# A step of a windowed attention stage in another order on four engines, and its masks laid by 32-row tiles

## The reference

```python
for i in range(DEPTH):                       # DEPTH = 6
    x = attn_layer(shift_tokens(x), Wqkv[i], q_scale[i], k_scale[i], Wo[i]) + x
    x = ffn_layer(shift_tokens(x), ln_g[i], ln_b[i], W1[i], b1[i], W2[i], b2[i]) + x

def attn_layer(x, Wqkv, qs, ksc, Wo):        # 16 heads of 64
    q, k, v = split(x @ Wqkv)
    q = l2norm(q) * qs;  k = l2norm(k) * ksc
    q = q * cos * scale + rotate_half(q) * sin * scale
    k = k * cos / scale + rotate_half(k) * sin / scale
    return local_attention(q, k, v) @ Wo

def local_attention(q, k, v):                # windows of 32 queries; keys: this window and the one before
    mask = (it < jb) | (it > jb + w) | (jb == -1)
    sim = einsum('bhwie,bhwje->bhwij', bq, bk2) * 8.0
    attn = softmax(where(mask, -max, sim))
    return einsum('bhwij,bhwje->bhwie', attn, bv2)
```

## Time and profile before

| | |
|---|---|
| median of three executions | 2125.77 us |
| profiled execution | 2125.36 us |
| its span | 2123.6 us |
| PE busy | 1930.0 us (91%) |
| PEld busy | 1456.1 us (69%) |
| DVE busy | 1688.3 us (80%) |
| ACT busy | 1421.5 us (67%) |
| POOL busy | 1246.3 us (59%) |
| mean granted clock of TensorE | 0.955 of full speed |

### The profile page before, as it was taken

How to read it: one execution, slowest core, us unless ns; L and a number is a source line. 1 busy time by engine, 2 the same in 40 slices (tenths; PEclk the granted TensorE clock), 3 DMA queues, 4 the chain that set the end, 5 groups by cost and what they waited for, 6 DMA issues and landing times. The chain is left out here.

```text
span 2123.6 us, 79458 instructions
## 1 busy us (share of the span) xinstructions
PE 1930.0 (91%) x33524; PEld 1456.1 (69%) x33524; DVE 1688.3 (80%) x3905; ACT 1421.5 (67%) x5112; POOL 1246.3 (59%) x871
## 2 busy tenths in 40 slices
PE   5779999999999999999999999999999995494496
PEld 3358778687786886868868778687686872252374
DVE  5679889698796996978969889698796965795654
ACT  4269779597795985968959779597695972342121
POOL 2268768388584885857858668587584851031000
PEclk9879999999999999999999999999999998696798
DMA  3011122031120211212112121021120110001000
GB/s 114 0 46 42 29 53 57 20 79 34 45 59 22 75 42 36 57 31 72 42 25 63 40 54 54 20 67 48 41 55 18 42 34 13 0 2 61 1 1 21
DMA packets 88229, 85.72 MB, mean 40 GB/s; under 512 B 15392, under 2 KB 83008, under 8 KB 87232
## 3 DMA queue, kind: packets, MB, share of 16 engines
q1 hardware_dynamic: 87872, 80.63, 13.8%
HBM read 25.51 MB, written 1.05 MB: 13 GB/s over the span
## 5 line engine op out<-in xcount | busy, mean ns | idle before, releaser
L1082 POOL TENSOR_TENSOR RN<-N,minus_half 128x8 f32<-128x8 f32 x384 | 632.7, 1648 | 168.8 <-DVE N L1010 168.8
L920 ACT ACTIVATE PB<-PS,NMX 128x64 f32<-128x64 f32 x1536 | 471.4, 337 | 29.9 <-DVE NMX L1030 29.8
L679 PE MATMUL PS<-WQ,XS 128*128 128x256 f32 x1536 | 436.2, 407 | 7.4 <-SPq L623 6.5
L920 ACT ACTIVATION_READ_ACCUMULATOR PB<-PS,NMX 128x1 f32 x1536 | 348.0, 227 | 0.0
L679 PEld LDWEIGHTS PS<-WQ,XS 128*128 128x128 f32 x1536 | 262.3, 190 | 44.9 <-SPq L623 6.9
L1077 POOL TENSOR_TENSOR RR<-R 128x512 f32<-128x512 f32 x192 | 244.9, 1275 | 78.3 <-DVE QK L1040 78.3
L903 ACT ACTIVATE QKT<-PS 128x512 f32<-128x512 f32 x384 | 229.5, 598 | 84.8 <-PE PS L765 84.7
L1077 POOL TENSOR_TENSOR RR<-R1B,R2B 128x512 f32<-128x512 f32 x192 | 245.0, 1276 | 69.2 <-DVE QK L1040 69.2
L1040 DVE SCALAR_TENSOR_TENSOR QK<-RN,RR 128x512 f32<-128x512 f32 x384 | 261.8, 682 | 0.6 <-POOL RR L1077 0.6
L1010 DVE TENSOR_REDUCE N<-SQ 128x8 f32<-128x512 f32 x384 | 259.6, 676 | 0.0
L886 ACT ACTIVATE SQ<-PS 128x512 f32<-128x512 f32 x384 | 236.5, 616 | 9.4 <-PE PS L679 9.2
(11 more groups left out here) (270 smaller groups left out, 3516.9 us busy)
## 6 DMA issues: line engine op xcount, KB each, us to landing
VS<-XB SPq DMA_DIRECT2D x384, 96.0 KB, 2.1
VS<-XB SPq DMA_DIRECT2D x288, 32.0 KB, 2.1
WQ<-in_wqkv SPq DMA_DIRECT2D x40, 192.0 KB, 2.6
WO<-in_wo SPq DMA_DIRECT2D x6, 512.0 KB, 3.9
XS<-XT SPq DMA_DIRECT2D x10, 256.0 KB, 3.3
XS<-XT SPq DMA_DIRECT2D x10, 255.8 KB, 4.1
BIG<-in_wgu SPq DMA_DIRECT2D x1, 2048.0 KB, 8.0
W<-in_w SPq DMA_DIRECT2D x6, 341.0 KB, 3.3
```

The costliest lines, as they stand in the source:

```text
L679: mm = nc.tensor.matmul(PQ[:, m % 2, j * 256:(j + 1) * 256], XSb[b][:, t0:t0 + P], WQ[:, pair * 384:pair * 384 + 256], start=True, stop=True)
L920: ex = nc.scalar.activation(PB[:, g % 2, u, :], SC[:, h, DH * t:DH * t + DH], ACT.Exp, bias=NMX[:, u:u + 1], accum_out=PSUMS[:, g % 2, u:u ...
L1082: nc.gpsimd.tensor_tensor(RN[:, g % 2, :], N2[:, g % 2, :], minus_half[:, :], ALU.pow)
```

## The change

Four edits, all in the steps of the attention block:

1. PE: `project_qk(g + 3)` moves from the head of the step to behind the values and the transposed probabilities, ahead of the masks.
2. PE: the mask is laid by 32-row tiles. For each of the two heads there were one matmul of 128 rows by 128 columns of the array; now there are four of 32 by 32, on the array's diagonal, each with its 32 rows of the identity and of the mask (8 in a step instead of 2). All four write the same PSUM bank, each its own 32 partitions.
3. ACT: the squares of unit g+3 go ahead of the copy of values and probabilities.
4. DVE: the sine product of unit g+2 goes ahead of the inverse of the softmax sums, and the product with the inverse norm (unit g+1) goes ahead of the normalisation of the probabilities and of the maxima.

```diff
@@ PE, step(g)
-                        if there(g + 3) and not tail:
-                            project_qk(g + 3)
                         if there(g):
                             pe.wait_ge(qk_in.sem, qk_in.take())
...
                         if values or probs:
                             last.then_inc(vp_ps.sem, 1)
+                        if there(g + 3) and not tail:
+                            project_qk(g + 3)
                         if tail:
                             down(1)
...
                             for h in range(2):
-                                nc.tensor.matmul(
-                                    SC[:, h, 0:P], identb[:, :],
-                                    bandmask[:, 0 if c == 0 else 1, :, :].rearrange("p t k -> p (t k)"),
-                                    start=True, stop=False)
+                                for w in range(4):
+                                    rows = slice(WIN * w, WIN * w + WIN)
+                                    nc.tensor.matmul(
+                                        SC[rows, h, 0:P], identb[rows, rows],
+                                        bandmask[rows, 0 if c == 0 else 1, :, :].rearrange("p t k -> p (t k)"),
+                                        start=True, stop=False)
@@ ACT, step(g)
+                        if there(g + 3) and not feed_forward_at(g - 1):
+                            squares(g + 3)
                         if values or probs:
                             cols = slice(0 if values else 256, 512 if probs else 256)
                             act.wait_ge(vp_ps.sem, vp_ps.take())
                             nc.scalar.activation(XB[:, g % CH, cols], PX[:, cols], ACT.Copy)\
                                 .then_inc(vp_in.sem, 1)
-                        if there(g + 3) and not feed_forward_at(g - 1):
-                            squares(g + 3)
@@ DVE, step(g)
-                        if there(g - 1):
-                            dve.wait_ge(sc_free.sem, g)
-                            nc.vector.reciprocal(RO[:, k, :], PSUMS[:, k, :]).then_inc(ro_in.sem, 1)
                         if there(g + 2):
                             nc.vector.tensor_tensor(
                                 R2s[g % 2].rearrange("p j g v d -> p (j g) v d"),
...
+                        if there(g - 1):
+                            dve.wait_ge(sc_free.sem, g)
+                            nc.vector.reciprocal(RO[:, k, :], PSUMS[:, k, :]).then_inc(ro_in.sem, 1)
+                        if there(g + 1):
+                            dve.wait_ge(rr_in.sem, rr_in.take())
+                            nc.vector.scalar_tensor_tensor(QKg[(g + 1) % 2], RN[:, (g + 1) % 2, :].unsqueeze(2)
+                                                           .to_broadcast([P, 8, DH]), 1e12, RRg,
+                                                           ALU.min, ALU.mult)\
+                                .then_inc(qk_in.sem, 1)
                         if there(g - 1):
                             dve.wait_ge(ro_in.sem, ro_in.take())
...
                         if there(g) and not tail:
                             maxima()
-                        if there(g + 1):
-                            dve.wait_ge(rr_in.sem, rr_in.take())
-                            nc.vector.scalar_tensor_tensor(QKg[(g + 1) % 2], RN[:, (g + 1) % 2, :].unsqueeze(2)
-                                                           .to_broadcast([P, 8, DH]), 1e12, RRg,
-                                                           ALU.min, ALU.mult)\
-                                .then_inc(qk_in.sem, 1)
```

## The result

The changed kernel takes 2152.36 us (median of four executions, 2151.83 to 2154.69) against 2125.56 of the kernel before: ratio 1.0128 (95% interval 1.011 to 1.0145), +26.8 us. The forecast was 2179 us with a range of 2160 to 2200. The direction was right, the size was twice too large, and the time lies outside the range. The kernel before was timed again beside each group of experiments, at 2125.46 to 2127.07 us, so a difference between two groups is good to 1 or 2 us.

The account below looks back on a forecast made before the run. PE was taken to be full: a fourth change of shape and the mask rounds add 0.14 us a step, all else 0; 384 x 0.14 = 53.8 us on 2125.36 gives 2179 us, range 2160 to 2200.

Parts of the forecast that it names:

- PE is full, a step is its work and three changes of shape: PE in a plain step before the change: 3.25 us, with no gaps but three of 0.14 to 0.15 us.
- ring of `QK` and the copy: Maxima, `QK`, transposes, copy, scores: nearly as long as PE's own work; the new order opens it, gaining nothing.
- A fourth change of shape, 0.09 to 0.10, behind the projection: PE between projection and 32 by 32 masks: the first mask load waits 0.09 to 0.10 us after the last stream.
- Two rounds of masks, the last start at 0.10: Masks on PE: four side by side per head, second round 0.08 us behind, last start 0.10 behind the first load.
- The first load of the step is exposed in either order: Head of PE's step: 0.11 us uncovered before projection or transposes alike, so the order changes nothing.
- 384 steps at one price: All steps, including the 11 feed-forward stretches and the tail: each pays the same 0.14 us, 53.8 us in sum.
- The range: Whole kernel: 384 x 0.09 = 35 to 384 x 0.19 = 73 us more, so 2160 to 2199, given as 2160 to 2200.
- ACT, DVE, POOL at nothing: The other engines' new orders and waits: PE waits for none of them, cost 0.
- one by one: Rival on the masks: a head's four run serially into one bank, 0.45 us a step, 2298 us; 10 in 100.
- No change: Rival: only going between whole and split array costs, so masks and scores share one drain, 2125.8 us; 6 in 100.
- Faster: Rival: the gap ahead of the scores is a wait for ACT's copy, 0.09 us a step less, 2091 us; 4 in 100.

Follow-up runs that it names:

- 64-row masks: The changed kernel with its eight masks laid as tiles of 64 rows by 32 columns, the shape of the scores: 2122.46 us.
- the order alone: The changed kernel with the masks laid as before, by two whole-array matmuls: 2108.81 us, ratio 0.992.
- output of 64 by 32: New order, masks of before, with the attention output in 64 by 32 tiles, twice as many matmuls: 2185.35 us, ratio 1.0274.

## Why the prediction was right or wrong, point by point

- **PE is full, a step is its work and three changes of shape**: right. Opening the ring of `QK` and the copy alone gave nothing (2125.28 us).
- **A fourth change of shape, 0.09 to 0.10, behind the projection**: right. The mask load comes 0.30 behind the last projection matmul, 0.216 of it stream. The Trainium skill's rule that a change of tiling mode drains the array ("TensorEngine Tiling (Array Packing)", Key Properties) holds for 32 by 32 too, and the 64-row masks show its other side: where masks and scores share a shape there is no gap between them.
- **Two rounds of masks, the last start at 0.10**: 0.08. The second round starts 0.065 behind the first, where the forecast took the 0.08 of the float32 scores. Together with smaller roundings the masks cost 0.109 a step where 0.14 was forecast, so 0.03 too much, some 12 us. Alone this would have left the time inside the range (384 x 0.109 = 42, 2167 us).
- **"The first load of the step is exposed in either order (0.97 - 0.86 = 0.11 before the projection, now before the transposes)"**: this is the step that failed. The exposure is real and the price of 0.11 was right for the projection (0.10 by the starts in the trace), but it was carried over to another kind of load. A transpose's costs 0.055 (0.49 - 0.44). So the order, put at nothing, gains 0.046 a step, and with the masks' 0.109 that leaves 0.063, where 0.14 was forecast. The evidence was there: the loads of the kernel before, by shape (busy us, mean ns, 450 to 650 us), had to be read for the transposes as well:

```profile
L679 PEld LDWEIGHTS PS<-WQ,XS 128*128 128x128 f32 x207 | 35.1, 189 | 4.7
L765 PEld LDWEIGHTS PS<-ident,QK 128*128 128x128 f32 x208 | 26.0, 141 | 5.7 <-issue 0.6
```

  The two differ by 0.048 us, and the two exposures, 0.102 and 0.055 by the starts, by 0.047. The Trainium skill ("TensorE: Matmul & The Clock Gate", LDWEIGHTS) gives a weight load columns / 1.2 ns; an estimate from it is 107 ns for 128 columns, for both kinds. The projection's exposure is near it, the transposes' 0.055 is half of it, and the measurement decides.
- **384 steps at one price**: not quite. The profiled execution of the changed kernel is 29.3 us longer than that of before (it was the slowest of its four, the medians differ by 26.8). The 372 distances between the masks of plain steps add 24.2, most of it 372 x 0.063 = 23.4. The 11 that hold a feed-forward went from 35.56 to 35.67 us, which adds 1.2: there the masks cost their 0.11, and the order gains nothing (35.56 with the order alone too). The last 4 us lie outside the steps, 2.5 ahead of the first mask and 1.4 behind the last. Their cause stays open.
- **The range** took its low end from the masks alone (0.09 a step) and held no doubt on the order, which was priced at exactly nothing. That zero was two prices that were taken to be equal.
- **ACT, DVE, POOL at nothing**: right for the whole. ACT's edit by itself changes nothing (2110.05 without it, 2108.81 us with it). DVE's is not idle: without it the same PE order takes 2351 us. The prediction said that `QK` would be 0.9 ahead of its transposes; it is 0.85.
- **Rivals**: one by one is refuted (0.112 a step for eight more masks, not 0.44). The Trainium skill's sentence that different row tiles cannot access one bank at a time ("TensorEngine Tiling (Array Packing)", Gotcha 1: PSUM Pressure) does not hold here for four tiles on the diagonal of the array, which write disjoint partitions of a bank. No change (shapes that split the columns count as one) is refuted by the 0.15 that still stands between the last mask and the scores' load. Faster (that gap is a wait for ACT) is refuted by the same 0.15, with the copy now ending 0.5 ahead, and by the orders of ACT and DVE alone (2125.28 us). The new order does gain 17 us, but by the load at its head.

## What to carry to other kernels

When PE is full, count its changes of array shape as instructions of their own, of 0.09 us each in this kernel, and look at what stands directly behind one: its first load is covered by nothing, so the cheapest kind of load belongs there, if what it waits for is early (with a late `XB` the values cost 0.15 us more there). Splitting a matmul into smaller tiles saves no stream if the columns streamed stay the same, and pays a change of shape unless both neighbours have that shape; before splitting further, look at how fast PE starts matmuls that have no pause ahead of them. And a cost put down as "the same before and after" is a difference of two prices: read both.

## What the runs showed of the hardware that was not expected

- The exposed first load behind a change of shape: 0.10 to 0.11 us ahead of float32 products of 128 columns, 0.055 ahead of float32 transposes.
- The burst of 32 small matmuls 0.007 us apart is seen behind a change of shape; without one the same 32 took 0.31 instead of 0.24 us (masks of 64 rows), and 64 of them in a row (output of 64 by 32) came 0.010 apart, with stops of up to 2.0 us on PE for which the profile shows no releaser.
- Four 32 by 32 tiles on the diagonal write one PSUM bank side by side: eight more such matmuls cost 0.112 us.
